# One tile, one group: reordering heads 0 to 2 of a two-layer graph attention kernel

## What is computed

```python
# layer 0
h = jnp.maximum(_layernorm(x, axis=-1), 0.0)
h = jnp.einsum('bnf,of->bno', h, W)
e = leaky_relu((h @ a_src)[:, :, None] + (h @ a_dst)[:, None, :])
e = jnp.where(adj == 0, NEG_INF, e)
x = x + jnp.einsum('bij,bjo->bio', softmax(e), h)
# layer 1: the same with four heads of 64 columns
logits = leaky_relu(s_src[:, :, None, :] + s_dst[:, None, :, :])
logits = jnp.where(adj_matrix[..., None] == 1, logits, NEG_INF)
out = jnp.einsum('bijh,bjhc->bihc', softmax(logits, axis=2), f)
```

## Time and profile before

| | |
|---|---|
| median of 3 runs | 2969.18 us (2967.61 to 2971.07) |
| profiled execution, its own time | 2966.78 us |
| its span | 2964.8 us |
| mean granted TensorE clock | 0.951 |
| TensorE busy with matmuls | 2591.2 us, 87% |
| VectorE / ScalarE / GpSimd busy | 2025.5 / 1731.7 / 1355.9 us |

### The profile page before, as it was taken

One profiled execution on the slowest core, in us unless ns is written; L12 is line 12 of the kernel. 1 busy time (PEld: TensorE's weight loads), 2 busy tenths in 40 slices (PEclk: granted clock), 3 DMA queues, 4 the chain that ended last, 5 costly groups with the idle time before them and its releaser, 6 DMA issues.

```text
span 2964.8 us, 64498 instructions
## 1 busy us (share of the span) xinstructions
PE 2591.2 (87%) x22950; PEld 2336.0 (79%) x22950; DVE 2025.5 (68%) x3326; ACT 1731.7 (58%) x3294; POOL 1355.9 (46%) x1759
## 2 busy tenths in 40 slices
PE   5987999879998799988999699987999979997687
PEld 4776888768887688867888588885888868886686
DVE  2458667586665766666667766768666586765996
ACT  4026566576665656657556566556666676664575
POOL 2113445434544444443455445553444535444566
PEclk9998999989999899998999899998999989998898
DMA  9330323203232033311323112331133302200000
GB/s 154 38 45 5 44 43 43 41 8 43 42 43 37 8 45 44 44 34 12 43 42 44 33 16 43 43 45 32 19 50 48 52 5 36 33 8 8 1 14 14
DMA packets 173749, 104.03 MB, mean 35 GB/s; under 512 B 140256, under 2 KB 140768, under 8 KB 173536
## 3 DMA queue, kind: packets, MB, share of 16 engines
q0 software_dynamic: 18432, 33.56, 13.8%
q1 hardware_dynamic: 155104, 67.79, 10.2%
HBM read 151.66 MB, written 16.78 MB: 57 GB/s over the span
## 4 chain that ended last, share of the span: by engine, by line
PE 65%; DVE 22%; issue 7%; ACT 4%; POOL 1%; DVEq 1%; DMA 0%; SPq 0%; ACTq 0%; POOLq 0%
PE accA L860 28%; PE accB L879 16%; PE accB L885 11%; PE accA L783 4%; DVE c L1117 4%; DVE shared L1004 2%; DVE shared L1137 2%; DVE xb L1106 2%; DVE Sw L1002 2%; PE accA L769 2%; PE misc_ps L758 2%; DVE xb L1099 1%; DVE shared L1072 1%; DVE stats L925 1%; DVE shared L999 1%
## 5 line engine op out<-in xcount | busy, mean ns | idle before, releaser
L661 ACT ACTIVATE shared<-Rb,w 128x512 int8<-128x512 f32 x1728 | 1086.4, 718 | 345.3 <-DVE shared L1137 344.9
L879 PE MATMUL accB<-Sw,shared 128*128 128x195 bf16 x7680 | 968.8, 248 | 77.9 <-DVE shared L1141 77.0
L860 PE MATMUL accA<-S,shared 128*128 128x257 f32 x4096 | 974.3, 391 | 53.4 <-DVE shared L1072 53.4
L860 PEld LDWEIGHTS accA<-S,shared 128*128 128x128 f32 x4096 | 771.4, 194 | 162.9 <-DVE shared L1072 61.7
L885 PE MATMUL accB<-Sv,shared 128*128 128x130 f16 x7680 | 757.9, 222 | 0.0
L879 PEld LDWEIGHTS accB<-Sw,shared 128*128 128x128 fp8e4 x7680 | 638.0, 98 | 118.0 <-issue 90.6
L1072 DVE SCALAR_TENSOR_TENSOR shared<-Rb,w,mask 128x512 f32<-128x512 f32 x512 | 432.5, 859 | 364.5 <-PE accA L860 319.8
L885 PEld LDWEIGHTS accB<-Sv,shared 128*128 128x128 fp8e4 x7680 | 572.3, 98 | 0.2
L1137 DVE TENSOR_TENSOR shared<-shared,mask 128x512 uint32<-128x512 uint32 x432 | 332.6, 770 | 232.4 <-ACT shared L661 222.9
L475 POOL TENSOR_SCALAR shared<-shared 128x260 f32<-128x260 f32 x128 | 135.9, 1062 | 757.5 <-ACT shared L719 757.5
L1141 DVE TENSOR_TENSOR shared<-shared,mask 128x512 uint32<-128x512 uint32 x512 | 392.9, 767 | 8.9
(11 more groups left out here) (107 smaller groups left out, 2569.4 us busy)
## 6 DMA issues: line engine op xcount, KB each, us to landing
adj_rows<-in_adj POOLq DMA_DIRECT2D x128, 256.0 KB, 5.4
xb<-in_x SPq DMA_DIRECT2D x32, 512.0 KB, 4.1
out<-xb SPq DMA_DIRECT2D x32, 512.0 KB, 2.8
mask<-adj_rows SPq DMA_TRANSPOSE x128, 4.3
shared<-in_W SPq DMA_DIRECT2D x2, 256.0 KB, 2.9
a_cols<-in_a SPq DMA_DIRECT2D x8, 0.2 KB, 10.4
bias<-in_b SPq DMA_DIRECT2D x1, 128.0 KB, 9.3
a_cols<-in_a_dst SPq DMA_DIRECT2D x1, 1.0 KB, 7.3
```

What stands on the lines that cost most here:

```text
L661: last = nc.scalar.activation(cmp[:, slot, jj // 2, of_pair(jj % 2, 0, CI)], Rb[:, h, :], ACT.Sign, bias=w[1][:, JG * g + jj, h:h + 1], sc ...
L860: last = nc.tensor.matmul(accA[:, k, 0:F + 1], tiles[:, j % RING, k * P:(k + 1) * P], S0[:, j, 0:F + 1], start=j == 0, stop=j == NJ - 1)
L879: nc.tensor.matmul(acc[:, bank, col:col + NS], bits[:, g % BRING, 1, jj // 2, of_pair(jj % 2, k * P, P)], Sw[:, j, h, :, :].rearrange("p a ...
```

## The change

Only the list for heads 0 to 2 changes. The list of the last head stays.

```diff
             if not last:
-                events += [a[0], a[1], g[0], g[1], a[2]] + load + [g[2], a[3]] + r + [g[3]] + eb
+                events += [a[0], g[0], a[1], g[1], a[2], g[2]] + load + [a[3]] + r + [g[3]] + eb
             else:
                 events += [a[0], a[1], a[2], a[3]] + ea + [g[0]] + ra + [g[1]] + load
                 events += [g[2]] + r + [g[3]] + x1 + eb
```

## The result

The changed kernel took 3004.43 us (median of 4 runs, 3001.29 to 3010.37), the kernel before 2969.12 us beside it. The ratio is 1.0121 with a 95% interval of 1.0101 to 1.0141: slower by 1.2%, 35 us. The profiled execution took 3001.33 us with a span of 2999.3 us, so the traces differ by 34.5 us. The four runs fall into two pairs, 3001.3 twice at a mean clock of 0.953, and 3007.5 and 3010.4 at 0.947; the clock term of the prediction varies from run to run.

What follows compares the result with a forecast made beforehand. TensorE, busy 87% of the span, was taken as the bound. A new copy-out wait of 33.6 us plus 3 us for the clock made 36.6, so about 3005 us, slower by 1.2%, range 2986 to 3024 us.

Steps and rivals of the forecast that it cites:

- the clock term: TensorE's clock falling behind head 0's gaps: 12 new falls cost 8.4 us, 3 old ones go for 5.0, net +3 us.
- The new wait in heads 1 and 2: TensorE's first group there waits for ScalarE's copy-out of the head before: 0.60 us at 56 places, 33.6 us.
- the hand-over: Ahead of that first group, from the end of ScalarE's copy to TensorE's start: 0.04 to 0.15 us.
- Head 0 costs nothing: In 21 chunks head 0's gaps are only divided anew, 1.45 + 2.08 into about 2.55 + 0.97 us: cost 0.
- Contention: In head 0, A1 beside GpSimd is up to 0.4 us slower, the first C0 gains as much: 0, bounds 8 us.
- The rival in which A1 is held for a whole operation of 1.1 us: In head 0 each A1 meets a whole GpSimd operation: 23 us on top, 3028 us; chance 5%.
- No new wait: In heads 1 and 2 ScalarE's copy isn't late, only the clock change is left: 2972 us; chance 7%.
- Head 0 gains: S of g(0,1) comes 0.66 us earlier in 21 chunks, 14 us gained: 2955 us without the copy wait; chance 5%.
- The clock costs in full: A fall behind each of head 0's 21 gaps, not covered by the following gap: 30 us on top, 3033; chance 6%.

Runs made afterwards that it cites:

- the split by heads: Two kernels, the new order in only some heads and the old one elsewhere: in head 0 only, 2964.57 us; in heads 1 and 2 only, 3020.12 us.
- the earlier copy: The changed kernel with ScalarE copying the sums out ahead of its comparison in heads 0 and 1: 2973.86 us, ratio 1.0027.
- the longer copy: Two more ScalarE copies in the copy-out of heads 0 and 1: 2967.52 us in the kernel before, 3048.97 us in the changed kernel.
- head 0 alone: The kernel before with the new order in head 0 only, the old one in heads 1 and 2: 2964.57 us, ratio 0.9995.
- heads 1 and 2 alone: The kernel before with the new order in heads 1 and 2 only, the old one in head 0: 3020.12 us, ratio 1.0176.

## Why the prediction was right

**The new wait in heads 1 and 2** was the cause, as forecast. Its count of 56 and its place were right, and three experiments bear on it: the split by heads, the earlier copy, and the longer copy. Its size was taken a little low: 0.60 us, measured 0.68 on average. The term that was mis-sized is the hand-over, with 0.04 to 0.15 us as its bounds; it measured 0.23 at most of the places (0.14 to 0.33). Both rows that bounded it were of other kinds, a ScalarE copy ahead of a transpose and a VectorE step ahead of a group. The split of a pair of tiles, 0.06 us, was not in the sum at all. The steps of 17.39 us from g(1,0) to g(2,0) (289.09 to 306.48 in the changed kernel) against 16.68 before (1441.93 to 1458.61) give 0.71 with that split, so 56 x 0.71 = 40 us where I had 33.6.

**Head 0 costs nothing.** Right, and shown alone (0.9995). I had treated 21 chunks as alike. In twelve of them the gaps came out at 2.30 and 1.04 us for 2.55 and 0.97, since TensorE's first group came 0.25 us sooner than I had it; in the other nine the first gap is 1.8 us. The group g(0,1) starts 9.56 us behind a0, or 10.0 where the clock fell, so on either side of the 9.7 that I had named.

**Contention.** I had taken 0, and where the clock didn't fall, S of g(0,1) came 0.13 us sooner, at most 3 us in all. A1 beside GpSimd took 1.13 us, so 0.4 more as in the earlier trace rows, and the first four instructions of C0 took 1.82 us in place of 2.35. The rival in which A1 is held for a whole operation of 1.1 us did not come: A1 would have taken some 1.8 us. That rival's price was misread. The 1.1 us of GpSimd's rows hold its own wait for VectorE; with VectorE idle the same operation took 0.65 us. In the changed kernel, first alone and then beside VectorE:

```profile
309.12 0.65 POOL L479 TENSOR_TENSOR shared<-shared 128x260 f32<-128x260 f32 x1
...
1508.78 1.02 DVE L1141 TENSOR_TENSOR shared<-shared,mask 128x512 uint32<-128x512 uint32 x1
1509.22 1.09 POOL L479 TENSOR_TENSOR shared<-shared 128x260 f32<-128x260 f32 x1
1509.73 1.13 DVE L1072 SCALAR_TENSOR_TENSOR shared<-Rb,w,mask 128x512 f32<-128x512 f32 x1
```

GpSimd's operation ended at 1510.31 and A1 at 1510.86, 0.55 us later. So did all 74 tiles of this trace that VectorE began inside one of GpSimd's operations of 256 elements or more, whatever the length of that operation: 0.545 to 0.551 us behind its end. A tile alone takes some 0.74 from its own start. It holds the other way round too: the 52 operations of L479 that began inside a tile, an N or an S ended 0.50 to 0.51 us behind its end. The trace agrees with the rule of the Trainium skill (SBUF — State Buffer, on the shared port pair): each looks fully blocked until the other engine's instruction is done. What A1 loses by it is only the rest of the operation that is under way, here 0.4 us.

**The clock.** This term was wrong. I had 12 new falls at 0.7 us less 3 old ones at 1.67, so +3 us. The trace has 5 falls in the chunks, at 0.46 each, so -2.7 us: the sum has the other sign, and 5 of 21 is far fewer than the half that I had named. It is luck that the total comes out so near. The new wait cost some 6 us more than forecast, and the clock some 6 us less: 40 - 3 - 3 = 34, beside 34.5 between the traces. What lies outside this sum nearly cancels. The time ahead of the first AB chunk is 3.1 us shorter, and about as much is added elsewhere, which I have not traced to a cause. The number of falls can't be read from the length of the gaps. Of the twelve gaps of 2.30 us in the second and third chunks of a phase, 5 were followed by a fall in the changed kernel, all 12 with head 0 alone, 10 with the earlier copy, and none with the longer copy. What decides it, no run here shows.

**The rivals.** "No new wait" is refuted by the L719 line. "Head 0 gains" needed S of g(0,1) 0.66 us sooner, and it came 0.13 sooner; head 0 alone gained nothing that can be told from noise. "The clock costs in full" did not come either: 5 falls of 21, and each covered but for 0.46 us. Falls at their full price came with heads 1 and 2 alone, nine of them, where g(0,1) is the first work behind the gap of 2.1 us.

What stays open: the run-to-run spread of the changed kernel (3001 to 3010 us) goes with its mean clock, 0.953 or 0.947. Only the first kind has a trace, so that the 6 to 9 us are falls is argued and not shown.

## What to carry to other kernels

When two streams share an engine, look at what each piece of one covers for the other: here the second tile in a row (1.76 us) hid the end of a copy-out that is queued on ScalarE behind a comparison. A table of waits doesn't list a wait that is covered, so take the releaser's end from the start of the instruction behind it: where that slack (here 1.28 us) is less than the piece that is moved away (1.76 us), the wait comes to light. And put the work that is cheap for the late engine and long for the bound one (here 0.66 against 1.76 us) where the late engine holds things up.

## What the runs showed of the hardware

- From the end of ScalarE's last copy to TensorE's next matmul it took 0.23 us at most of the 56 places (0.14 to 0.33) when the wait stands ahead of a bf16 group, and 0.04 us at the one place ahead of a transpose.
- A fall of TensorE's clock to half cost 1.6 to 1.9 us where a busy stretch followed, and 0.46 us where a wait of 1 us for VectorE came behind it. Nine falls with heads 1 and 2 alone so cost some 15 us, and the five of the changed kernel 2 us.
- A tile that VectorE began inside a GpSimd operation of 256 elements or more ended 0.55 us behind the end of that operation, in all 74 cases of the changed kernel, whether that operation took 0.7 us or 2.2.
- VectorE's compare with one tensor as its source (L1117) took 2.52 us for four beside GpSimd (at 1510.78 in the changed kernel) in place of 1.67 with GpSimd idle (at 1352.19 in the kernel before).
